# Cross-attention block on one core: the second tile's row maximum and the row normalisation moved behind the last probabilities' low parts, TensorE's first transposes in one run

## The reference

```python
xq  = layer_norm(x, qn_w, qn_b);  ctx = layer_norm(context, cn_w, cn_b)
q   = (xq @ q_w).reshape(B, N, H, D);  k, v = split(ctx @ kv_w)
attn = einsum('bnhd,bmhd->bhnm', q, k) * scale
attn = where(xa_mask, -max, attn);  attn = softmax(attn, -1)
x = x + einsum('bhnm,bmhd->bnhd', attn, v).reshape(B, N, C) @ proj_w + proj_b
h = gelu(layer_norm(x, n2_w, n2_b) @ fc1_w + fc1_b) @ fc2_w + fc2_b
return x + h
```

## Time and profile before

| | us |
|---|---|
| median of 3 runs | 1140.06 (1139.83 to 1140.64) |
| the profiled execution, its own time | 1140.32 |
| its span, first to last instruction | 1138.5 |
| TensorE busy | 1108.1 (97%) |
| VectorE busy | 584.1 (51%) |
| ScalarE busy | 407.2 (36%) |
| GpSimd busy | 231.5 (20%) |
| mean granted TensorE clock | 0.997 |

### The profile page before, as it was taken

The page is one execution under the profiler, slowest core; times in us unless marked ns, Lnnn a source line. Parts: engine busy times, 40 slices in busy tenths (PEclk is TensorE's granted clock), DMA queues, the critical chain, the costliest instruction groups (busy, mean ns, idle before and its releaser), DMA issues.

```text
span 1138.5 us, 16382 instructions
## 1 busy us (share of the span) xinstructions
PE 1108.1 (97%) x5849; PEld 943.0 (83%) x5849; DVE 584.1 (51%) x1154; ACT 407.2 (36%) x1158; POOL 231.5 (20%) x186
## 2 busy tenths in 40 slices
PE   4999999999999999999999999999999999999998
PEld 4789888998899888888888888888888888888887
DVE  7888878888888865633323322322332333232212
ACT  3456665566666754421311321221221131121110
POOL 2343435434554420100100100100110110010000
PEclk9899999999999999999999999999999999999999
DMA  7011111222111025202002002002001000100101
GB/s 245 8 36 58 38 38 38 70 86 77 39 48 48 29 68 164 74 19 74 1 1 75 1 2 74 1 1 74 1 1 53 23 1 34 41 1 1 38 1 37
DMA packets 40144, 48.76 MB, mean 43 GB/s; under 512 B 10965, under 2 KB 19197, under 8 KB 40087
## 3 DMA queue, kind: packets, MB, share of 16 engines
q1 hardware_dynamic: 37919, 43.74, 11.7%
q10 hardware_dynamic: 2168, 4.21, 1.0%
HBM read 30.54 MB, written 16.78 MB: 42 GB/s over the span
## 4 chain that ended last, share of the span: by engine, by line
PE 87%; DVE 8%; issue 2%; ACT 2%; DVEq 0%; POOL 0%; ACTq 0%; POOLq 0%
PE bank L1311 31%; PE bank L1282 31%; PE bank L1193 8%; PE bank L1151 5%; PE bank L1182 4%; PE bank L1132 3%; PE bank L1164 2%; DVE bnst L886 1%; DVE S L833 1%; PE bank L1294 1%; DVE PTl L863 1%; DVE nmax L840 1%; ACT S L642 1%; PE bank L1142 1%; PE bank L1109 1%
## 5 line engine op out<-in xcount | busy, mean ns | idle before, releaser
L1311 PE MATMUL bank<-w,gTh 128*128 128x512 f32 x1024 | 319.2, 393 | 0.0
L1052 DVE CAST gTh<-g 128x512 fp32r<-128x512 f32 x128 | 56.9, 444 | 442.8 <-ACT g L744 442.8
L744 ACT ACTIVATE g<-bank,cols 128x512 f32<-128x512 f32 x128 | 88.0, 688 | 471.5 <-PE bank L1282 470.0
L1311 PEld LDWEIGHTS bank<-w,gTh 128*128 128x128 f32 x1024 | 192.4, 188 | 42.7
L1311 PE MATMUL bank<-w,gTl 128*128 128x512 f32 x512 | 200.4, 391 | 0.0
L1282 PE MATMUL bank<-hT0h,w 128*128 128x512 f32 x512 | 162.1, 397 | 0.0
L1282 PE MATMUL bank<-hT1h,w 128*128 128x512 f32 x512 | 159.1, 392 | 0.1
L480 POOL TENSOR_TENSOR hrs<-hve,mhalf 128x1 f32<-128x1 f32 x32 | 17.6, 549 | 555.2 <-DVE hve L1026 555.2
L1311 PEld LDWEIGHTS bank<-w,gTl 128*128 128x128 f32 x512 | 96.1, 188 | 22.0
L1282 PEld LDWEIGHTS bank<-hT0h,w 128*128 128x128 f32 x512 | 94.7, 188 | 21.5
L1282 PEld LDWEIGHTS bank<-hT1h,w 128*128 128x128 f32 x512 | 95.1, 188 | 19.9 <-issue 0.5
(11 more groups left out here) (103 smaller groups left out, 1809.5 us busy)
## 6 DMA issues: line engine op xcount, KB each, us to landing
xr<-in_x SPq DMA_DIRECT2D x16, 512.0 KB, 3.5
x_scratch<-xr SPq DMA_DIRECT2D x16, 512.0 KB, 2.8
x<-x_scratch SPq DMA_DIRECT2D x8, 1024.0 KB, 5.5
out<-x SPq DMA_DIRECT2D x7, 1024.0 KB, 4.3
w1raw<-in_L_xattn_fc_w SPq DMA_DIRECT2D x16, 256.0 KB, 3.0
w2raw<-in_L_xattn_fc_w SPq DMA_DIRECT2D x16, 256.0 KB, 2.7
kvw<-in_L_xattn_kv_w ACTq DMA_DIRECT2D x2, 1024.0 KB, 10.5
qraw<-in_L_xattn_q_w ACTq DMA_DIRECT2D x1, 1024.0 KB, 11.2
```

The costliest lines, as they stand in the source:

```text
L744: act.activation(g[:, :], bF[j % 2][:, :], ACT.Gelu, bias=cols[:, F1B + j:F1B + j + 1]).then_inc(a_gelu.sem, 1)
L1052: dve.tensor_copy(gT[HI][j % 4][:, :], g[:, :]).then_inc(v_ghi.sem, 1)
L1311: mm = pe.matmul(bC[t][:, :], gT[d][j % 4][:, t * P:(t + 1) * P], w2[:, j, w, :], start=(j == 0 and i == 0), stop=(j == JT - 1 and i == 2))
```

## The change

In passes that have `prep` equal to None (0 to 14, where their parts exist), `maximum(1)` leaves its place ahead of `av_lo(0)`, and `normed` its place ahead of `av_lo(1)`. Both now stand behind `prob_lo(3)`, in the order `normed`, `maximum(1)`, and ahead of `h_normed` and `av_lo(2)`. On TensorE the two scores, the two `x_T` and the first `prob_T` of a pass are grouped: two scores, all the transposes, two scores. No instruction is added or removed.

```diff
 # VectorE
-            if scores:
+            if scores and prep is not None:
                 maximum(1)
...
             if front:
                 q_lo(0)
+            if prep == "q":
+                proj_weights(range(1, KT))
+            if back:
+                av_lo(1)
+                prob_lo(3)
             if norm and prep is None:
                 normed()
-            if prep == "q":
-                proj_weights(range(1, KT))
-            if back:
-                av_lo(1)
-                prob_lo(3)
+            if scores and prep is None:
+                maximum(1)
             if norm2 is not None:
                 h_normed(static(0), norm2)
 # TensorE
             if scores and prep is None:
                 score(0, 0)
+                score(0, 1)
             if front and prep is None:
                 x_T(0)
-            if scores and prep is None:
-                score(0, 1)
-            if front and prep is None:
                 x_T(1)
             if back:
-                prob_T1(0, 0)
+                prob_T(0)
             if scores and prep is None:
                 score(0, 2)
-            if back:
-                prob_T1(0, 1)
-            if scores and prep is None:
                 score(0, 3)
```

More of the change, by code:

```diff
@@ L972, in step @@
                 q_lo(0)
-            if norm and prep is None:
-                normed()
             if prep == "q":
@@ L979, in step @@
                 prob_lo(3)
+            if norm and prep is None:
+                normed()
+            if scores and prep is None:
+                maximum(1)
             if norm2 is not None:
```

## The result

The changed kernel takes 1134.03 us (median of 5, 1133.25 to 1134.14) against 1140.06; the ratio is 0.9945, interval 0.9930 to 0.9959. It is 6.0 us faster, where 7.3 had been forecast; 1132.8 us was expected. The profiled execution took 1134.04 us with a span of 1132.3.

What follows compares the result with a forecast made beforehand. TensorE was taken to set the pace, stalling three times a pass behind VectorE, the second bound. Gains of 8.2 (loop) and 0.5 less 1.4 (pass 14) made 7.3 us: 1132.8 from 1140.06, range 1128.2 to 1137.8.

Steps and rivals of the forecast that it cites:

- ten loop passes: Loop: each pass gains 0.82 us by the earlier start of `proj(0)`, 8.2 us in all.
- passes 10 to 12: Passes behind the loop, mostly led by VectorE: gain 0.17 us each, 0.5 in all; between loss 0.2 and gain 0.6.
- pass 13: Nothing to gain; loses up to 0.17 us at `q(0)`, swallowed by pass 14's waits.
- pass 14: Loses 1.4 us: `proj(0)` 0.52 later behind `maximum(1)`, 0.84 more from `w1_lo` beside L525.
- The stalls ahead of `prob_T(3)` and `av(3)`: TensorE waits on VectorE's `prob_lo(2)` and `prob_lo(3)`, 1.11 and 0.18 us a loop pass; both go.
- The new wait at `proj(0)`: In the loop, `proj(0)` waits for VectorE's `av_lo(2)`, ending at 191.04: 0.30 us a pass.
- 191.92 - 191.10 = 0.82: Old less new start of `proj(0)` in a loop pass, taken as the pass's gain: 0.82 us.
- TensorE's order: Grouped transposes end `x_T(0)` one score later; the stall at `q(0)` grows by 0.17 us a pass.
- the 1.78 named as a sign: Sign in a loop pass: `q(0)` at about 1.78 us, against 1.61 before.
- `av(0)` waits for `prob_lo(1)`: Step for passes 10 to 12: `av(0)` at 9.20 us into the pass, so VectorE gets 0.5 us idle time.
- The port: Rival, passes 10 to 13: L525 goes first and `h_normed` waits 2.2 us; 1140.9 us, no difference; chance 0.05.
- The ring: Rival: GpSimd path from `maximum(1)` to `prob_T1(0,1)`, 0.2 us slack, comes late; slower, 1145.8 at 1.0 us; chance 0.09.

Runs made afterwards that it cites:

- The two half-changes: VectorE's half alone and TensorE's half alone, each on the kernel before: 1131.84 us and 1142.35 us.
- TensorE's half alone: The kernel before with only TensorE's transposes grouped, VectorE's order old: 1142.35 us, ratio 1.0019.

## Why the prediction was right, point by point

| term | forecast, us | measured, us |
|---|---|---|
| start of pass 0 | 0 | -0.4 (55.08 to 54.72) |
| ten loop passes | -8.2 | -6.7: -0.86 in pass 0, -0.645 each in passes 1 to 9 |
| passes 10 to 12 | -0.5 | -1.7 (23.97 to 23.40 each) |
| pass 13 | +0.17, swallowed | +0.17 |
| pass 14 | +1.4 | +2.06 |
| behind it | 0 | +0.2 |
| sum | -7.3 | -6.3 of span (1138.53 to 1132.25), -6.0 of the medians |

The total is nearer than its terms, and that is luck: the loop gained 1.5 us less than forecast and pass 14 lost 0.7 more, while passes 10 to 12 gained 1.2 more, by a wait that I had misread.

- **The stalls ahead of `prob_T(3)` and `av(3)`** go in full, 1.29 us. Right; what was not said is that `maximum(1)` alone would do it, and that `normed` is needed for neither.
- **The new wait at `proj(0)`** is there, and VectorE's path to `av_lo(2)` is what makes it. In the second pass shown `proj(0)` starts 17.15 us behind the pass's opening, where the forecast had 17.14 (191.10 less 173.96). In every other pass ScalarE's copy after `x_T(0)` begins 0.09 later and it is 17.25.
- **Too small a price for a wait.** The sum counted the time until `proj(0)` starts, not the 0.11 us that the first step behind it is longer, because its first weights are not loaded ahead. With half of the 0.09 this explains the loop: 0.82 - 0.11 - 0.05 = 0.66 against 0.645 measured. What the prediction mis-sized is thus the term "191.92 - 191.10 = 0.82": it took the difference of the two starts of `proj(0)` for the whole gain.
- **TensorE's order costs**, forecast at 0.17 us a pass. The two half-changes put it at 0.20 (23.63 less 23.43, and 22.79 less 22.60), 2.2 us in all. Right in sign and cause: it is the place of `x_T(0)`, which starts 0.85 us into a pass instead of 0.42, while `x_T(1)` starts at 1.28 or 1.29 in both orders. The last matmul of `q(0)` starts 0.16 or 0.26 later, in turn from pass to pass, 0.2 on the mean; in the chain `q(0)` takes 1.70 us, not the 1.78 named as a sign, because it begins later as well.
- **Passes 10 to 12** gained 0.57 each, not 0.17. The step that failed: "`av(0)` waits for `prob_lo(1)`". In the code it waits for `prob_lo(0)`. In pass 10 it starts 8.71 us into the pass, not 9.20, and the 0.5 us of idle time that I had put ahead of `av_lo(1)` does not exist.
- **Pass 14**: 0.83 for `w1_lo` behind L525 (forecast 0.84) and 0.62 for `maximum(1)` (forecast 0.52, plus 0.11 for the restart). The first `w1_lo`, 0.61, was missing.
- **The port** at `h_normed`: it did not decide, since `h_normed` starts ahead of L525 (300.91 against 301.06 in pass 10). L525 is the one that pays: it takes 2.48 us in passes 10 to 13, where it took 2.25. The exchange of `normed` and `maximum(1)` shows that the price in that rival was about right, 2.08 us of waiting at `proj(0)` against 2.2.
- **The ring** had its slack, 0.33 us from the end of L536 to `prob_T1(0,1)` where 0.2 had been worked out, and no more: with `maximum(1)` one instruction further back it sets the pace.

The first row and the last but one are scatter as far as the traces tell. Pass 0 opens between 54.23 and 55.44 us in the twelve traces of this case, and what follows `proj(1)` of pass 15 takes 717.57 to 717.88 us; the kernel before and the changed one lie inside both ranges. Pass 0 itself takes 25.15 and 25.14 us in the kernel before and in TensorE's half alone, and 24.29 in the changed kernel.

## What to carry to other kernels

When an instruction moves on an engine without gaps, write down what must be finished for each consumer: a move past a consumer helps it by the instruction's length at most, and any consumer for which it still stands in front gains nothing and becomes the next wait. Before grouping instructions to save switches, look whether the rows show a cost of switching at all, and which engine feeds on the results one by one. Look what GpSimd does beside each element-wise VectorE instruction on SBUF, above all right behind the VectorE instruction that releases GpSimd: here the order of two neighbours was worth 34 us.

## What the runs showed of the hardware

With `normed` and `maximum(1)` exchanged, TensorE's granted clock fell in six of the passes (1, 4, 6, 8, 10 and 11). Windows of two neighbouring passes, and TensorE's timeline behind the wait at `proj(0)`:

```profile
182.85:207.54 24.69, 22.52 (x162) 21.06 (x160) 20.84 (x40) 13.66 (x51) 9.02 (x6) 1.00 0.13 43
207.54:233.91 26.37, 24.14 (x162) 22.24 (x161) 20.95 (x40) 13.67 (x51) 11.99 (x10) 0.94 0.12 41
```

```profile
226.72 0.50 PE L1195 MATMUL bank<-wph,aTh 128*128 128x512 f32 x1 [2.08 <-DVE aTl L868]
...
227.29 0.39 PE L1195 MATMUL bank<-wph,aTl 128*128 128x512 f32 x1
...
228.30 0.63 PE L1195 MATMUL bank<-wph,aTl 128*128 128x512 f32 x1
228.72 0.63 PE L1195 MATMUL bank<-wph,aTh 128*128 128x512 f32 x1
```

After 2.08 us of idling the steps from matmul to matmul are 0.34 us at the restart, then 0.23 us, the 2.4 GHz level, and then, over some eight matmuls, 0.43 us, the 1.2 GHz level. The mean granted clock of the pass is 0.94, and it is 1.68 us longer. The next pass, with the same idle time, keeps its clock. So a stall of 2.1 us cost up to 3.8 here. In the loop of the kernel before, where TensorE lost 1.11 us ahead of `prob_T(3)` in each pass, the windows show 1.00 throughout.
